# Prelude folded into the attention block, three layer-norm groups moved up, and the banks, order and waits of the local blocks regrouped

## What is computed

```python
mod = (_silu(c) @ wmod).reshape(2, 6, 1, -1)          # sa, ca, ga, sb, cb, gb
h = _layernorm(x) * (1 + ca) + sa
x = x + ga * attn(h)          # L0: delta attention, L1: causal linear attention and MLP
h = _layernorm(x) * (1 + cb) + sb
x = x + gb * ffn(h)           # ffn: 6 (L0) or 2 (L1) local-attention layers:
...
# one local layer, heads 16 or 8 of 64, window 32 or 64
q, k, v = split(shift(x) @ Wqkv); q = l2norm(q) * qs; k = l2norm(k) * ks; rotary(q, k)
x = x + softmax(mask(q @ [k_prev, k].T * 8)) @ [v_prev, v] @ Wo
hg = layernorm(shift(x)) * g + b @ W1 + b1; a, gate = split(hg)
x = x + a * gelu(gate) @ W2 + b2
```

## Time and profile before

| | us |
|---|---|
| median of 3 runs | 5260.22 (5258.66 to 5263.18) |
| profiled execution | 5259.56 |
| its span | 5257.8 |
| stretch 0 to 735 (front, attention, feed) | 735 |
| stretch 735 to 4090 (local block L0) | 3355 |
| stretch 4090 to 4390 (linear block) | 300 |
| stretch 4390 to 5258 (local block L1, residual) | 868 |

### The profile page before, as it was taken

How to read it: one execution, slowest core, us unless ns; L and a number is a source line. 1 busy time by engine, 2 the same in 40 slices (tenths; PEclk the granted TensorE clock), 3 DMA queues, 4 the chain that set the end, 5 groups by cost and what they waited for, 6 DMA issues and landing times. The chain is left out here.

```text
span 5257.8 us, 220614 instructions
## 1 busy us (share of the span) xinstructions
PE 4656.7 (89%) x81616; PEld 3372.6 (64%) x81616; DVE 3876.4 (74%) x8260; ACT 3195.5 (61%) x6716; POOL 2753.1 (52%) x3917
## 2 busy tenths in 40 slices
PE   3558948999999999999999999999999576999996
PEld 2556736676767666676767666767676454666665
DVE  5984567777777777777777777777777566777775
ACT  1002526677777777677777677777776344777675
POOL 0004116666666666666666666666665325555552
PEclk6996979999999999999999999999999688999998
DMA  1000125554545454555454555455554003444442
GB/s 58 17 1 18 43 57 130 137 132 134 132 130 139 127 143 127 141 131 141 128 141 128 140 131 140 129 136 133 138 134 119 17 7 87 115 113 114 114 113 77
DMA packets 704914, 564.32 MB, mean 107 GB/s; under 512 B 223492, under 2 KB 629864, under 8 KB 704008
## 3 DMA queue, kind: packets, MB, share of 16 engines
q1 hardware_dynamic: 691080, 537.36, 38.5%
q10 hardware_dynamic: 13312, 22.02, 1.3%
HBM read 359.38 MB, written 200.02 MB: 106 GB/s over the span
## 5 line engine op out<-in xcount | busy, mean ns | idle before, releaser
L2134 POOL TENSOR_TENSOR L_qk<-L_cos_part,L_sin_part 128x512 f32<-128x512 f32 x896 | 1128.7, 1273 | 151.5 <-DVE L_sin_part L2012 151.0
L1797 ACT ACTIVATE L_squares<-L_ps_q 128x512 f32<-128x512 f32 x896 | 534.8, 597 | 929.2 <-PE L_ps_q L1539 922.6
L1539 PE MATMUL L_ps_q<-L_w_qkv,L_xT 128*128 128x512 f32 x1792 | 971.9, 625 | 30.0 <-DVE L_sin_part L2012 11.1
L2125 POOL TENSOR_TENSOR L_qk<-L_qk,L_rnorm 128x1024 f32<-128x1024 f32 (+1 forms) x512 | 864.0, 1688 | 17.8 <-POOL L_rnorm L2108 0.5
L1574 PEld LDWEIGHTS L_ps_t<-L_ident,L_qk 128*128 128x128 f32 x3584 | 446.1, 141 | 479.1 <-issue 374.5
L2011 DVE TENSOR_TENSOR L_cos_part<-L_ps_q,L_rot 128x512 f32<-128x512 f32 x896 | 611.0, 682 | 41.2 <-POOL L_rot L2144 31.2
L2012 DVE TENSOR_TENSOR L_sin_part<-L_ps_q,L_rot 128x512 f32<-128x512 f32 x896 | 610.9, 682 | 0.0
L2013 DVE TENSOR_REDUCE L_sumsq<-L_squares 128x8 f32<-128x512 f32 x896 | 606.7, 677 | 0.0
L2102 POOL TENSOR_TENSOR L_nw_a<-L_rnorm 128x32 f32<-128x32 f32 (+1 forms) x256 | 59.5, 232 | 993.7 <-ACT L_rnorm L1827 993.7
L1574 PE MATMUL L_ps_t<-L_ident,L_qk 128*128 128x128 f32 x3584 | 540.2, 274 | 4.4 <-POOL L_qk L2125 3.2
L1808 ACT ACTIVATE L_qkT<-L_ps_t 128x512 f32<-128x512 f32 x896 | 530.6, 592 | 15.8 <-PE L_ps_t L1574 15.7
(11 more groups left out here) (290 smaller groups left out, 8908.2 us busy)
## 6 DMA issues: line engine op xcount, KB each, us to landing
...
v_rows<-L_val SPq DMA_DIRECT2D x384, 260.0 KB, 2.1
v_rows<-L_val SPq DMA_DIRECT2D x512, 65.0 KB, 2.0
L_rot_base<-in_rot SPq DMA_DIRECT2D x256, 128.0 KB, 2.1
v_rows<-L_val SPq DMA_DIRECT2D x128, 130.0 KB, 2.1
L_x_in<-x_rows SPq DMA_DIRECT2D x512, 32.0 KB, 1.7
mid_rows<-z SPq DMA_DIRECT2D x256, 64.0 KB, 1.6
L_f_in<-mid_rows SPq DMA_DIRECT2D x256, 64.0 KB, 2.0
```

The lines of the kernel that those rows point to most:

```text
L1539: nc.tensor.matmul(ps_q[j % 2][:, :], xT[:, parity(t), :], w_qkv[:, 0:2, 256 * j:256 * j + 256], start=True, stop=True).then_inc(S["proj_p ...
L1797: nc.scalar.activation(squares[:, j % 2, :], ps_q[j % 2][:, :], ACT.Square).then_inc(S["sq_done"], 1)
L2125: nc.gpsimd.tensor_tensor(v, v, r, ALU.mult).then_inc(S["normed"], 1)
L2134: nc.gpsimd.tensor_tensor(qk[:, t % 2, h, s, :], cos_part[:, j % 2, :], sin_part[:, j % 2, :], ALU.add).then_inc(S["added"], 1)
```

## The change

The two first blocks go away: the clearing of rows and the modulation are done inside the first block of `delta_attention_stage`, with c and the weights loaded first and x behind them on a semaphore of its own; two wide ScalarE copies and four wide VectorE instructions over all eight banks take the place of 48. The sum over keys waits for half the copies at a time. In the linear block statistics, roots and normalising of groups 0 to 2 are done in rounds i = 5, 6, 7 of the first loop. In the local blocks the transposed probabilities go to columns 256 to 512 of the two `ps_s` banks; `scores` waits for `prob_copy` and the last q and k copy before its masks; and the order of steps moves as below. A wait for `consts_in` in `scores` goes away too.

```diff
+                            sp.dma_start(c_in[:, 2 * l + b:2 * l + b + 1], c_rows[l][b, :].rearrange("(p o) -> p o", o=1)).then_inc(mod_in, 16)
...
+                        sp.dma_start(xr[:, 16 * b:16 * b + 16, :], x_dram[b].rearrange("(t p) d -> p t d", p=128)).then_inc(x_in, 16)
...
-                    pe.wait_ge(loaded, 144)
+                    pe.wait_ge(mod_in, 96)
+                    pe.wait_ge(wide_done, 1)
+                    for k in range(4):
+                        for j in range(2):
+                            last = nc.tensor.matmul(ps[2 * k + j][:, 0:384], wide[:, k, :], w_m[:, k // 2, 384 * j:384 * j + 384], start=True, stop=True)
+                    last.then_inc(product, 1)
+
+                    pe.wait_ge(loaded, 112)
+                    pe.wait_ge(mods_done, 6)
...
-                    act.wait_ge(loaded, 144)
+                    act.wait_ge(mod_in, 96)
+                    nc.scalar.activation(c_exp[:, :], c_in[:, :], ACT.Exp, scale=-1.0).then_inc(exped, 1)
+                    act.wait_ge(product, 1)
+                    by_part = mods[:, :, :, :].rearrange("p k (j i) d -> p (k j) i d", i=3)
+                    nc.scalar.activation(by_part[:, :, 0, :], banks[:, :, 0:128], ACT.Copy).then_inc(mods_done, 1)
+                    nc.scalar.activation(by_part[:, :, 1, :], banks[:, :, 128:256], ACT.Copy, bias=1.0).then_inc(mods_done, 1)
...
-                    dve.wait_ge(loaded, 144)
...
+                    dve.wait_ge(x_in, 32)
                     group_stats(nc, dve, step, xr, mean, rstd, (st, mv, var, half, tmp))
+                    dve.wait_ge(mods_done, 2)
+                    raw = banks[:, :, 256:384]
+                    nc.vector.tensor_scalar(sign, raw, 0.0, 2.0, ALU.is_ge, ALU.mult).then_inc(mods_done, 1)
+                    nc.vector.tensor_scalar(mag, raw, -1.0, 0.25, ALU.mult, ALU.max).then_inc(mods_done, 1)
+                    dve.wait_ge(mods_done, 4)
+                    step(nc.vector.scalar_tensor_tensor(mag, raw, 0.25, mag, ALU.max, ALU.max))
+                    nc.vector.scalar_tensor_tensor(mods[:, :, :, :].rearrange("p k (j i) d -> p (k j) i d", i=3)[:, :, 2, :], sign, -1.0, mag, ALU.add, ALU.mult).then_inc(mods_done, 2)
+                    dve.wait_ge(mods_done, 6)
...
-                    dve.wait_ge(k_out, SUB)
...
+                        dve.wait_ge(k_out, SUB // 2 * (j + 1))
...
+                    if i - 5 in EARLY_MID:
+                        normalise_mid(i - 5)
...
+                    early = i - 5
+                    if early in EARLY_MID:
+                        dve.wait_ge(S["mid_done"], early + 1)
+                        statistics(4, four(xm, early))
+                    if live(i + 1) or live(i + 3) or early in EARLY_MID:
+                        roots(0, i + 3, 0 if live(i + 1) else 4, 8 if live(i + 3) or early in EARLY_MID else 4, S["roots_a"])
...
+        ps_d = ps_q[0][:, 0:256] if NS == 2 else ps_x[:, 256:512]
...
+        P_VIEW = ps_s[:, :, 256:512].rearrange("x b (i q) -> x b i q", i=2)
...
+                def ready_to_project(k, T, hf):
+
+                    t, h = item(T, hf, AT_PROJ)
+                    if live(k, t):
+                        pe.wait_ge(wq_in[h], reloads(k, t, 16))
+                        wait(pe, S["rotated"], steps_(k, t, NS * h - 2))
...
-                        pe.wait_ge(S["xT_done"], tiles_(k, t))
-                        if s == 0:
-                            pe.wait_ge(wq_in[h], reloads(k, t, 16))
-                        wait(pe, S["rotated"], steps_(k, t, j - 2))
+                        if j == 0:
+                            pe.wait_ge(S["xT_done"], tiles_(k, t))
+                        if s:
+                            wait(pe, S["rotated"], steps_(k, t, j - 2))
...
-                        if j % 2 == 0:
+                        if j == 0:
                             wait(pe, S["mid_done"], tiles_(k, T - TO_OUT - 1))
+                        if NS == 2 and j == 2 and parity(T) == TO_FT % 2:
+                            wait(pe, S["new_done"], groups_(k, T - TO_DOWN))
...
-                            wait(pe, S["pT_done"], halves(k, t - 1, h - 1))
+                            wait(pe, S["qkT_done"], steps_(k, t, j - 1))
...
                     if live(k, t):
                         pe.wait_ge(v2_in[parity(t)][h], turns(k, t, 16 * V2_LOADS))
-                        if NS == 2:
-                            wait(pe, S["qkT_done"], steps_(k, t + 1, NS * h + NS - 1))
-                        else:
-                            wait(pe, S["oT_done"], halves(k, t, h - 1))
-                        wait(pe, S["pT_done"], halves(k, t, h - 1))
+                        read, g = item(T, hf, AT_SOFTMAX)
+                        if live(k, read):
+                            pe.wait_ge(S["shifted"], halves(k, read, g))
                         pe.wait_ge(S["exp_done"], halves(k, t, h))
                         for i in range(4):
-                            last = nc.tensor.transpose(ps_t[2 - NS][:, 128 * i:128 * i + 128], probs[:, h, 128 * i:128 * i + 128], ident[:, :])
+                            last = nc.tensor.transpose(P_VIEW[:, i // 2, i % 2, :], probs[:, h, 128 * i:128 * i + 128], ident[:, :])
...
-                        wait(pe, S["shifted"], halves(k, t, h - 1))
+                        v, g = item(T, hf, AT_PV)
+                        if live(k, v):
+                            pe.wait_ge(S["pT_done"], halves(k, v, g))
+                            wait(pe, S["att_done"], halves(k, v, g - 1))
+                        else:
+                            wait(pe, S["shifted"], halves(k, t, h - 1))
+                        pe.wait_ge(S["qkT_done"], steps_(k, t, NS * h + NS - 1))
...
-                        pe.wait_ge(S["pT_done"], mine)
-                        wait(pe, S["att_done"], before)
+                        s, _ = item(T, hf, AT_SCORE)
+                        if not live(k, s):
+                            pe.wait_ge(S["pT_done"], mine)
...
-                            if made == "up_ps":
-                                wait(pe, S["pT_done"], halves(k, item(T, 0, AT_PV)[0], item(T, 0, AT_PV)[1]))
+                            if made == "up_ps" and NS == 2:
+                                t, h = item(T, 0, AT_SCORE)
+                                wait(pe, S["qkT_done"], steps_(k, t, NS * h + NS - 1))
+                            elif made == "up_ps":
+                                t, h = item(T, 0, AT_OUT)
+                                wait(pe, S["oT_done"], halves(k, t, h))
...
-                        value_bank_read(k, T, 0)
+                        if NS == 2:
+                            t, h = item(T, 0, AT_PROJ)
+                            wait(pe, S["rotated"], steps_(k, t, NS * h))
+                            wait(pe, S["mid_done"], tiles_(k, T - TO_OUT - 1))
+                        else:
...
+                                last = nc.tensor.matmul(ps_d[:, 128 * j:128 * j + 128], hidden[0:n, c, 128 * j:128 * j + 128], w_down[0:n, c, :],
...
+                    if NS == 2:
+                        project(k, T, hf, 1)
                     out_transposes(k, T, hf)
                     if NS == 2:
-                        project(k, T, hf, 1)
                         qk_transposes(k, T, hf, 1)
+                        prob_transposes(k, T, hf)
                     values(k, T, hf)
...
                         up_projections(k, T, (0,))
                     if goes_down and early:
                         feature_transposes(k, T)
-                        down_projection(k, T)
                     if hf == 1 and early:
                         input_transpose(k, T)
-                    prob_transposes(k, T, hf)
+                    if early:
+                        prob_transposes(k, T, hf)
+                    if goes_down and early:
+                        down_projection(k, T)
...
                         if not early:
                             input_transpose(k, T)
                     if goes_down and not early:
+                        down_projection(k, T)
                         feature_transposes(k, T)
-                        down_projection(k, T)
+                    ready_to_project(k, T + hf, 1 - hf)
...
                 def emit(k, T, hf):
                     square(k, T, hf, 0)
                     qk_copy(k, T, hf, 0)
+                    if NS == 2:
+                        square(k, T, hf, 1)
                     out_copy(k, T, hf)
                     if hf == 0:
                         roots(k, T)
                     if NS == 2:
-                        square(k, T, hf, 1)
                         qk_copy(k, T, hf, 1)
                     if hf == 0 and T % 2 == TO_UP % 2:
                         exponentials(k, T, hf)
+                        if NS == 1:
+                            prob_copy(k, T, hf)
                         if live(k, T - TO_UP):
                             nc.scalar.preload_act_table_set("gelu_and_others")
```

(8 more changed lines are left out.)

141 lines of the change are left out of this document (48 added, 93 removed).

## The result

The changed kernel takes 5357.02 us (5350.98 to 5360.64, 4 runs) against 5260.16 beside it: ratio 1.0183, 95% interval 1.0167 to 1.0200. It is slower by 97 us, where 54 less had been forecast.

The account below looks back on a forecast made before the run. TensorE was taken to bound most of the kernel (busy 89%), but not the front and linear block. Terms -34 - 13 - 26 + 19 = -54 gave 5206 us; own range 5160 to 5240, 8-in-10 range 5110 to 5252.

Parts of the forecast that it names:

- The front: Kernel start up to the six-layer block: earlier x and overlapped sum over keys give -34 us, bounds -27 and -36.
- its first term: Front: x issued earlier, statistics starting at 13 to 15.4, first `h` at 34.2 instead of 63.62: -29.4 us.
- the sum over keys: Front: first half of the sum runs while the other half's copies are made, hiding 4.6 us: -4.6.
- The linear block: Between L0 and L1: statistics, roots and normalising of group 0 leave the gap: -13 us, bounds -19 and -5.
- the 8.5 us at worst: Linear block: up to 8.5 us come back if the moved small VectorE steps all fall beside GpSimd instructions.
- L0, down and plain slots: Six-layer block, two of four half-slots per period: freed bank wait and earlier second projection, -.42 and -.25 us.
- L0, norm slot: Six-layer block, half-slot where ScalarE runs `normalised`: masks must wait for `prob_copy`, +.54 us a period.
- The "-14" of the period: Six-layer block: the four slots together give -.15 us a period, times 96 periods, -14 us.
- The pass boundaries: Six-layer block, 11 boundaries: moved projection fills TensorE's 1.29 us wait for the attention, -1.0 each, -12 in all.
- L1: Two-layer block: norm slot +.65, up +.21, down -.24, plain -.03, together +.59 x 32 = +19 us, bounds +5 and +27.
- scores behind `prob_copy` cost more than all else wins: Rival, local blocks: masks wait for the probability copy in every slot; +75 to +110, 5280 to 5315 us; 7 in 100.
- The rival's threshold: The `prob_copy` rival decides the sign when costing over 73 us above the norm-slot prices, .57 a period over 128 periods.

Follow-up runs that it names:

- old_bank: Changed kernel with the transposed probabilities back in their earlier bank, behind the values, with the earlier waits; other moves kept: 5307.13 us, ratio 1.0083.
- order_back: Changed kernel with the six-layer block's earlier order of projection, transposes, values and second square; new bank and its waits kept: 5232.13 us, ratio .9951.
- copy_before_values: Changed kernel with ScalarE's exponential and `prob_copy` ahead of `val_copy` and `normalised`, six-layer block only: 5208.61 us, ratio .9901.
- prelude_only: Changed kernel with `local_block_stage` of the kernel before, so only front and linear block are changed: 5224.85 us, ratio .9926.

## Why the prediction was wrong

**The front** came near by two misses that cancel in part: x was in use 4.0 us later than the estimate (statistics at 17.03, past the prediction's upper bound of 15.4), so its first term is 25.3 and not 29.4; the sum over keys won 5.5 and not 4.6; and .9 more was won behind them. -31.7 for -34. **The linear block** held, -15.7 for -13: the dear VectorE step beside GpSimd (1.11 in the prediction's rows) came twice in the changed first loop, 1.17 and 1.18 us, and not as often as the 8.5 us at worst had it.

**L0, down and plain slots: the step that failed.** The prediction had the transposes of the probabilities freed from the wait of `ps_t0` and everything behind them earlier: -.42 and -.25. It saw that values move behind them and charged that to the norm slot alone, as .29. It did not see that the values lose their time to the second projection's move: their bank `ps_t1` is read by ScalarE (`outT`) later than before, and *old_bank* has them as late without the transposes ahead. The values come .60 later in these two slots (3.14 to 3.74 and 3.11 to 3.71), and *order_back* gives it back, masks included: .61 in the down slot, .44 in the plain one. That lateness reaches the masks by two paths. One is ScalarE's program, which has the values' copy ahead of the exponential and the copy of the probabilities, for which the scores now wait: *copy_before_values* leaves the values where they are, and the masks come .30 earlier in the down slot (6.74 to 6.44) and .23 in the plain one (6.86 to 6.63). What is left, .31 and .21, comes along TensorE's own order behind the values: in the plain slot the input transpose stands .21 later than in *order_back* (6.22 to 6.43), and *old_bank* shows this path without any wait of the scores for a copy. The move of the order costs 114 to 120 us; I had booked none for it. Measured were -.07 and +.12 a period, 70 us off the forecast over 96 periods.

**L0, norm slot: right mechanism, wrong size.** Masks behind the copy: +.54 forecast, +1.03 measured. The values were .40 later, not .29, and the signal, which I chose as .2, was .54, for five sequencer steps stand behind the late wait. With the .04 by which the copy ended behind the masks before, these make .98. That is another 47 us off the forecast.

**L0 as a whole.** The "-14" of the period was -.15; over all slots it came out at +.95, which holds the boundaries too.

**The pass boundaries** (-12): their wait is gone from the view of waits, and the up slot in which it stood is 1.06 us shorter (10.79 to 9.73), where -1.0 was forecast. With the new bank and the old order it is 10.53, so .80 of it comes with the moved order. Part is given back five slots later, in a norm slot that takes 9.72 at the boundaries and 9.19 elsewhere (8.24 and 8.26 before).

**L1:** +19 forecast, +43.5 measured. The norm slot gave +1.03 for +.65. Its masks' wait is the .91 of the prediction, but the signal behind it was .39; and the prediction's own terms, .91 and a signal of .2 less .3, make .81 and not the .65 it took. The ordinary up slot gave +.23 for +.21; two boundary slots gave 7 us more, which the prediction doesn't have. The down slot won .11 and not .24. Some 9 of the 43 appear also with L1's code unchanged (prelude_only), in part at these same boundary slots.

**The rivals.** That scores behind `prob_copy` cost more than all else wins was given 7 in 100, at 5280 to 5315; the measured time is 42 above even that. Its side of zero and its place are what happened, in part: the wait bites in the norm slot and, through the late values, in down and plain. It was priced as a copy's length a period more; the runs give 13 to 19 us for bank and wait in L0, and 114 to 120 for the order, which no rival had. (The rival's threshold doesn't follow either: by the forecast of -54 the sign turns at 54 us more, not at 73.) The Trainium skill's "PSUM bank collisions raise a hardware error" (PSUM - Partial Sum Buffer), by which columns 256 to 512 aren't free of the scores' bank, is the reason for the wait in `scores`; no run here shows a collision. The wait's cost is the 93 waits above, and its effect was smaller than the order's.
